# Merging VectorE instructions and taking the router's weights from a tanh, in a fused RWKV and mixture-of-experts kernel

## What is computed

```python
def step(carry, kv_t):
    aa, bb, pp = carry
    kt, vt = kv_t
    ww = u + kt
    p = jnp.maximum(pp, ww)
    e1 = jnp.exp(pp - p)
    e2 = jnp.exp(ww - p)
    y = (e1 * aa + e2 * vt) / (e1 * bb + e2)
    ww2 = pp + w
    p2 = jnp.maximum(ww2, kt)
    e1 = jnp.exp(ww2 - p2)
    e2 = jnp.exp(kt - p2)
    return ((e1 * aa + e2 * vt, e1 * bb + e2, p2), y)
# init: aa = 0, bb = 0, pp = -1e38, for each sequence
```

```python
logits = (xf @ Wr + br) / TAU            # TAU = 1.5
top_val, top_idx = jax.lax.top_k(logits, 2)
top_w = jax.nn.softmax(top_val, axis=-1)
yr = sum over the two experts of top_w * expert(x)
```

## Time and profile before

| what | before |
|---|---|
| median of 3 runs | 450.01 us (448.95 to 451.0) |
| span of the profiled execution | 471.4 us |
| busy: TensorE matmul | 399.7 us (85%) |
| busy: VectorE | 312.4 us (66%) |
| busy: ScalarE | 295.7 us (63%) |
| busy: GpSimd | 256.0 us (54%) |
| VectorE instructions | 1065 |
| mean granted TensorE clock | 0.947 of full speed |

### The profile page before, as it was taken

One profiled execution on the slowest core, in us unless ns is written; L12 is line 12 of the kernel. 1 busy time (PEld: TensorE's weight loads), 2 busy tenths in 40 slices (PEclk: granted clock), 3 DMA queues, 4 the chain that ended last, 5 costly groups with the idle time before them and its releaser, 6 DMA issues.

```text
span 471.4 us, 9935 instructions
## 1 busy us (share of the span) xinstructions
PE 399.7 (85%) x2503; PEld 307.2 (65%) x2503; DVE 312.4 (66%) x1065; ACT 295.7 (63%) x715; POOL 256.0 (54%) x328
## 2 busy tenths in 40 slices
PE   0566799998978988988593799999999999999991
PEld 0224466756746564664240369999999999999830
DVE  3799989999997997724560345656666665666162
ACT  2586699989796865663310237677777776777055
POOL 5666747567567857875566004444444444444264
PEclk9978799999999999997977699999999999999997
DMA  5389700000003000110122257876777776763394
GB/s 152 90 192 375 231 1 0 2 1 1 2 6 108 32 19 31 41 49 24 48 66 65 79 176 252 286 248 245 259 249 259 241 261 237 261 230 126 102 333 124
DMA packets 51471, 64.86 MB, mean 138 GB/s; under 512 B 8924, under 2 KB 35292, under 8 KB 51416
## 3 DMA queue, kind: packets, MB, share of 16 engines
q1 hardware_dynamic: 46968, 54.85, 35.1%
q0 software_dynamic: 4448, 9.38, 6.1%
HBM read 21.65 MB, written 13.91 MB: 75 GB/s over the span
## 4 chain that ended last, share of the span: by engine, by line
PE 51%; DVE 20%; issue 8%; SPq 6%; ACT 5%; POOL 4%; DMA 2%; another core or an unknown queue 2%; DVEq 0%; ACTq 0%; POOLq 0%
PE bank L1280 21%; PE bank L1298 11%; PE bank L987 4%; DVE rec L555 3%; DVE bst L475 2%; PE bank L969 2%; SPq L1087 2%; SPq L1086 2%; ACT z L690 2%; PE bank L1272 2%; PE bank L998 2%; PE bank L999 1%; PE bank L920 1%; POOL frs L821 1%
## 5 line engine op out<-in xcount | busy, mean ns | idle before, releaser
L1141 POOL DMA_INDIRECT routed_rows<-yo,goes_to x75 | 71.8, 957 | 112.8 <-DVE yo L1190 110.4
L1280 PE MATMUL bank<-xT,w 128*128 128x128 f32 x900 | 113.3, 276 | 0.6 <-ACT xT L1228 0.4
L1280 PEld LDWEIGHTS bank<-xT,w 128*128 128x128 f32 x900 | 106.6, 192 | 1.1 <-ACT xT L1228 0.5
L1182 DVE SCALAR_TENSOR_TENSOR actT<-bank,tile_bias,gl 128x128 f32<-128x128 f32 x225 | 65.3, 345 | 24.8 <-ACT gl L1234 15.1
L403 POOL DMA_INDIRECT dispatched_rows<-rows_all,slot_i x64 | 63.4, 990 | 22.7 <-issue 17.4
L1234 ACT ACTIVATE gl<-bank,tile_bias 128x128 f32<-128x128 f32 x225 | 65.9, 364 | 14.1 <-PE bank L1280 7.6
L1298 PE MATMUL bank<-we_sb,actT 128*128 x450 | 62.9, 276 | 1.0 <-DVE yo L1190 1.0
L1298 PEld LDWEIGHTS bank<-we_sb,actT 128*128 128x128 f32 x450 | 56.1, 192 | 1.6 <-issue 1.4
L1190 DVE SCALAR_TENSOR_TENSOR yo<-bank,goes,wb 128x128 f32<-128x128 f32 x75 | 26.3, 350 | 37.5 <-PE bank L1298 34.5
L1228 ACT ACTIVATE xT<-bank 128x128 f32<-128x128 f32 x75 | 20.8, 277 | 26.2 <-PE bank L1272 24.2
L969 PE MATMUL bank<-xk,wfk_sb 128*128 128x512 f32 x64 | 33.0, 626 | 4.9 <-DVE xk L572 3.8
(11 more groups left out here) (201 smaller groups left out, 778.4 us busy)
## 6 DMA issues: line engine op xcount, KB each, us to landing
w<-we_sb SPq DMA_DIRECT2D x75, 384.0 KB
x_all<-dispatched_rows SPq DMA_DIRECT2D x75, 68.0 KB
we_sb<-we SPq DMA_DIRECT2D x1, 4608.0 KB
rows_all<-x SPq DMA_DIRECT2D x8, 256.0 KB, 2.9
x_all<-routed_rows SPq DMA_DIRECT2D x8, 256.0 KB, 4.9
rows_all<-routed_rows SPq DMA_DIRECT2D x8, 256.0 KB, 5.3
out<-x_all SPq DMA_DIRECT2D x8, 256.0 KB, 2.5
routed_rows<-yo,goes_to POOLq DMA_INDIRECT x75
```

The lines of the kernel that those rows point to most:

```text
L1141: ng.indirect_dma_start(routed, bass.IndirectOffsetOnAxis(ap=goes_to[n // U % DB][:, n % U:n % U + 1], axis=0), yo[n % YO][:, :], None).th ...
L1182: nv.scalar_tensor_tensor(actT[n % UA][:, at], ps_a[j][:, 0:P], tile_bias[:, j, n:n + 1], gl[n % 2][:, at], ALU.add, ALU.mult).then_inc(s2 ...
L1280: return nt.matmul(to[:, 0:P], w1[m][:, off:off + P], xT[m][:, :], start=True, stop=True)
```

## The change

The change does two things. First, tiles are laid out so that pairs of operands lie side by side: the four exponentials become one tile e_all of 4x512, of which the middle two are the factors that multiply v, and the state tile ab loses its gap between the two sequences of a chunk. With that `weigh_v` issues one product of 128x1024 in place of two of 128x512, `states` issues two scans of 512 in place of four of 256 (running over the boundary between the two sequences, where the factor on the old state is zero), and `carried` issues one product of 128x1024 in place of two. Second, ScalarE takes tanh of half the difference of the logits and writes it to column DW of the rows, since the difference of the two weights is that tanh; VectorE makes W0 as 0.5 - 0.5 DW in one instruction in place of a sum, a reciprocal, a product and a difference. Nothing is moved in the order of any engine.

```diff
-        ab = tmp("ab", [P, 2, SQ, T + 1])
+        ab = tmp("ab", [P, 2, W + 1])
         gap = tmp("gap", [P, 2, W])
-        e_plus = tmp("e_plus", [P, 2, W])
-        e_minus = tmp("e_minus", [P, 2, W])
+        e_all = tmp("e_all", [P, 4, W])
+        e_plus, e_minus = e_all[:, 0:2, :], e_all[:, 2:4, :]
+        new_parts = e_all[:, 1:3, :]
...
-        e2v = tmp("e2v", [P, W])
-        new_v = tmp("new_v", [P, W])
+        weighed = tmp("weighed", [P, 2, W])
+        new_v, e2v = weighed[:, 0, :], weighed[:, 1, :]
...
             v.wait_ge(s["rel_ready"], b + 1)
-            routed_by(nv.tensor_scalar(total[:, 0:m], rel[:, 0:m], 1.0, None, ALU.add))
-            routed_by(nv.reciprocal(rows_all[:, lo:hi, W0], total[:, 0:m]))
-            routed_by(nv.tensor_tensor(w_second[:, 0:m], rel[:, 0:m], rows_all[:, lo:hi, W0], ALU.mult))
-            nv.tensor_tensor(rows_all[:, lo:hi, DW], w_second[:, 0:m], rows_all[:, lo:hi, W0], ALU.subtract)
+            nv.tensor_scalar(rows_all[:, lo:hi, W0], rows_all[:, lo:hi, DW], -0.5, 0.5, ALU.mult, ALU.add)
             v.wait_ge(s["prefix_ready"], b + 1)
...
-            nc.scalar.activation(rel[:, 0:m], fall[:, 0:m], ACT.Exp, scale=1.0 / TAU).then_inc(s["rel_ready"], 1)
+            lo, hi = BATCH[b][0] * CT, BATCH[b][1] * CT
+            nc.scalar.activation(rows_all[:, lo:hi, DW], fall[:, 0:m], ACT.Tanh, scale=0.5 / TAU).then_inc(s["rel_ready"], 1)
...
-                nv.tensor_tensor(e2v[:, :], new_in_state, pv[:, :], ALU.mult)
-                nv.tensor_tensor(new_v[:, :], new_in_output, pv[:, :], ALU.mult).then_inc(s["ev_ready"], 1)
+                nv.tensor_tensor(weighed[:, :, :], new_parts, under(pv[:, :], 2), ALU.mult).then_inc(s["ev_ready"], 1)
...
-                for q in range(SQ):
-                    at = slice(q * T, (q + 1) * T)
-                    nv.tensor_tensor_scan(ab[:, 0, q, 1:T + 1], old_in_state[:, at], e2v[:, at], 0.0, ALU.mult, ALU.add)
-                    last = nv.tensor_tensor_scan(ab[:, 1, q, 1:T + 1], old_in_state[:, at], new_in_state[:, at], 0.0,
-                                                 ALU.mult, ALU.add)
-                last.then_inc(s["states_ready"], 1)
+                nv.tensor_tensor_scan(ab[:, 0, 1:W + 1], old_in_state, e2v, 0.0, ALU.mult, ALU.add)
+                nv.tensor_tensor_scan(ab[:, 1, 1:W + 1], old_in_state, new_in_state, 0.0, ALU.mult, ALU.add).then_inc(s["states_ready"], 1)
...
-                for n in range(2):
-                    last = nv.tensor_tensor(by_sequence(nd[:, n, :]), ab[:, n, :, 0:T], by_sequence(old_in_output), ALU.mult)
-                last.then_inc(s["nd_ready"], 1)
+                nv.tensor_tensor(nd[:, :, :], ab[:, :, 0:W], under(old_in_output, 2), ALU.mult).then_inc(s["nd_ready"], 1)
```

More of the change, by code:

```diff
@@ L134, in build @@
         fall = sb("fall", [P, BT])
-        rel = sb("rel", [P, BT])
-        total = sb("total", [P, BT])
-        w_second = sb("w_second", [P, BT])
         slot = sb("slot", [P, K, BT])
@@ L416, in attention_vector @@
             nv.memset(pp[:, :, 0:1], NEG)
-            nv.memset(ab[:, :, :, 0:1], 0.0)
+            nv.memset(ab[:, :, 0:1], 0.0)
             nv.memset(ones_bf[:, :], 1.0)
@@ L872, in add_new @@
                 ng.tensor_tensor(nd[:, 1, :], nd[:, 1, :], new_in_output, ALU.add).then_inc(s["den_half"], 1)
-                ng.tensor_tensor(nd[:, 0, :], nd[:, 0, :], new_v[:, :], ALU.add).then_inc(s["den_ready"], 1)
+                ng.tensor_tensor(nd[:, 0, :], nd[:, 0, :], new_v, ALU.add).then_inc(s["den_ready"], 1)
             def residual(c):
```

## The result

The changed kernel takes 452.21 us (median of 6 runs, 450.84 to 454.61), the kernel before 450.15 us on the same chip (6 runs, 448.95 to 451.13). The ratio is 1.0052, with an interval of 1.0030 to 1.0075: slower by about half a per cent, or 2.1 us, where 449.6 was predicted.

A forecast was written before the change was run, and what follows sets the result against it. No single engine was taken to bound the chunks before the experts: TensorE to 73 us, both TensorE and VectorE to 101.2, then VectorE fuller. 1.35 + 1.2 - 2.1 = 0.45 us gained, 450.01 to 449.6 us; range 446.8 to 452.2.

The forecast's parts named there:

- Part 1: Eight VectorE instructions a chunk become four: 0.07 us a merge, 2.1 us over eight chunks, 1.35 us on the path.
- Part 2: In placed, one VectorE instruction for four saves 0.64 us in each of four batches; 1.2 us counts.
- Its split over the batches: Gain from the tanh in placed: 0.3 us at batch 0, 0.3 at 1, 0 at 2, 0.64 at 3.
- pricing the loads at about nothing: Four ScalarE table loads go, 5.1 us, but are hidden by other waits: 0, with a bound of 1.3 us.
- Part 3: Longer scans hold off GpSimd's third norm at chunks 0, 2, 4 and 5: 2.1 us lost, bounds 0 and 3.3.
- The covers that I named: Slack hiding part of the third norm's delay after chunk 0: 0.3 us left at chunk 2, 0.6 at 4, 0 at 5.
- TensorE is not waiting there: At chunk 2, the reason the third norm's delay is partly covered: 0.3 us lost.
- 32 matmuls ahead: At chunk 5, TensorE's queued work covers the third norm's delay: 0 us lost.
- (b): Wait on GpSimd counts in all three chunks, 3.3 us, against 0.6 gained: 452.7 us, slower; chance 0.18.
- (a): Wait on GpSimd costs nothing that counts: 2.55 us gained, 447.5 us, at best 446.2; chance 0.32.
- (c): Merges do nothing and the tanh alone acts, with no delay: 1.2 us gained, 448.8 us; chance 0.12.
- pauses without a releaser: Unexplained waits in the profiled execution's chain, such as 2.46 us at 228.89, said to lie all after 205 us.

The follow-up runs named there:

- free_scans: Changed kernel with scans merged in chunks 0, 2, 4 and 7 only, four of 256 in the others; 447.15 us, ratio 0.9933 to the kernel before.
- held_3: free_scans with the scans merged in chunk 3 too; 470.27 us, ratio 0.9950 to the kernel before.
- tanh_only: Kernel before with only the weights made from one tanh; 473.33 us, ratio 0.9971 to the kernel before.
- held_5: free_scans with the scans merged in chunk 5 too; 470.17 us, ratio 0.9946 to the kernel before.
- held_6: free_scans with the scans merged in chunk 6 too; 470.35 us, ratio 0.9951 to the kernel before.
- after_weigh_between: Changed kernel, all scans merged, with weigh_v moved from ahead of stats2 to behind it at two places; 452.39 us, ratio 1.0054 to the kernel before.
- scans_only: Kernel before with only its scans merged, in the changed kernel's tile layout; 479.83 us, ratio 1.0101 to the kernel before.
- held_scans: Changed kernel with scans merged in chunks 1, 3, 5 and 6 only; 454.04 us, ratio 1.0092 to the kernel before.
- held_1: free_scans with the scans merged in chunk 1 too; 471.36 us, ratio 0.9974 to the kernel before.

## Why the prediction was wrong, step by step

**Part 1, the merges**: the sizes hold nearly. Two products as one save 0.06 us (a step of 1.14 from 49.74, against twice 0.60), forecast 0.07; two scans as one save 0.03 to 0.05 (47.33 to 48.44, 1.11, against twice 0.57; from the first scan to the instruction behind the last, four take 2.32 us in `free_scans` and two 2.23 in held_3), forecast 0.06. The sum of parts 1 and 2 was 2.55 us; `free_scans`, which has all of them but the merges at four places, gains 0.67% or 3.0 us. **Part 2, the tanh**: 1.2 forecast, 1.4 measured with an interval from -0.1 to 2.9. Its split over the batches isn't borne out: by x1c of chunk 5, behind batch 0, `tanh_only` is 1.6 us ahead of the kernel before (144.52 and 146.09), where it was 0.25 ahead at chunk 4 and 0.3 was forecast for this batch. No table load came back and no wait took their place, so pricing the loads at about nothing isn't contradicted, though no run takes them away alone.

**Part 3** is the term that failed, by its second half. Its first half, that a scan holds GpSimd off for its whole length, gave 1.0 and 1.9 us for operations that took 1.02 and 1.84, and 1.2 us for a delay of 1.29. Its second half, what that delay costs, was set at 1.2, 0.3, 0.6 and 0 for the places at chunks 0, 2, 4 and 5, 2.1 in all. The traces show 1.20 at chunk 2, 1.21 at chunk 4 and 1.24 at chunk 5 (held_3, held_5, held_6), and the whole is 5.3 us by the time of chunk 7, 3.9 at the end of the same two executions, and 6.3 in the medians. The covers that I named were there: at chunk 2 the norm's delay reaches `mix` as 0.30 us. That this is the very number predicted is luck: it was set without a row. I stopped at that number. What is late next is VectorE, and GpSimd's operations over 128x512 hold VectorE off just as VectorE's scans hold GpSimd: it was enough that `mix` came 0.18 us behind GpSimd's sum instead of ahead of it. "TensorE is not waiting there" and "32 matmuls ahead" were answers about TensorE, while in these stretches VectorE was the fuller of the two, as I had read from the earlier trace rows. For chunk 5 the 0, a full cover, was wrong for the same reason: x3c waited for both of GpSimd's additions.

The Trainium skill (SBUF — State Buffer, Who interferes with whom) calls what VectorE and GpSimd share an exclusive lock. I cited it for one direction and priced that one only. Both directions are in the rows above (1.27 to 1.65 for GpSimd, 0.74 to 1.64 for VectorE), and the PSUM case of `after_weigh_between` agrees with it too.

The sum with what was measured: gains of 3.0, a loss of 3.9 to 6.3, net 0.9 to 3.3 slower; the two comparisons of the whole change gave 2.1 and 3.1. **Of the rivals**, (b) was nearest in its time (452.7) and its sign, and it named the places; but its price of 3.3 us was at most the delay of the norm in three chunks, and it was four places with the hold on VectorE added. (a) is refuted by `free_scans`, which is what (a) forecast (447.5) once the held places are taken out. (c) is refuted by `scans_only` and `held_scans`. One reading was wrong without an effect on the sum: not all pauses without a releaser lie behind 205 us, the chain of the kernel before has one of 0.84 us at 147.35. The range ended at 452.2, just under the 452.21 measured, because its upper end took in only part of (b).

**What stays open.** Between the 5.3 us at chunk 7 and the 6.3 of the medians lie what happens behind chunk 7 (the same two executions end only 3.9 apart) and the spread of the runs; they aren't told apart. The place at chunk 0, for which 1.2 us was forecast, wasn't priced: held_1 loses 2.7 us there, with a longer stretch at the low clock than `free_scans` (53.2 to 60 us against 52.5 to 55.6). Why VectorE loses even when its record starts first (by 0.02 us at chunk 0, by 0.26 in held_6) isn't shown either. The traces of before and after differ by only 1.1 us at chunk 7 (187.97 and 189.06), and before that by -1.5 at chunk 0; TensorE's stretches at 1.2 GHz fall at other moments in each kernel (at 42.7 us in the kernel before, for one, and not in the kernel after), and no run holds them fixed.

## What to carry to other kernels

Before merging VectorE instructions that read two operands from SBUF, look at what GpSimd does beside them: a merge of two scans saved about 0.05 us, and doubling the length for which GpSimd is shut out delayed the next chunk by 1.2 us at each of the three places that were measured one by one, where GpSimd carried a norm that others wait for. Merge where GpSimd is idle or busy with long work, and leave the short form where it isn't; here this gave 447.15 us against 450.42 and 453.49. And follow a delay beyond its cover: ask not only whether the next engine waits, but whether two engines that exclude each other now start in the other order.

## What the runs showed of the hardware

- The hold works both ways: of the same pair, GpSimd's sum took 1.65 us and `mix` 0.74 when VectorE led by 0.22 us, and 1.27 and 1.64 when GpSimd led by 0.18. The order of the recorded starts doesn't always tell who is held: right behind another operation of GpSimd, its addition at 55.03 in the kernel after held `mix`, recorded from 55.01 on (1.85 us).
- A VectorE instruction can be held through two operations that follow each other on GpSimd: x3c, recorded from 151.58 on in held_6, took 3.33 us, through two additions of 1.28 us (from 151.84 on). It isn't always so: in the kernel after, `mix` got in behind the first one and ended at 56.86, and GpSimd's next operation, from 56.26 on, took 1.72 us.
- Not every operation of GpSimd holds VectorE: in `free_scans` `mix` took 0.75 us (from 53.93 on) within a power of 128x4 (53.74 to 54.76), and in held_6 0.74 us (from 154.83 on) within a row scatter (154.51 to 155.76).
- A VectorE product with one operand in PSUM leaves GpSimd its full speed: 0.20 and 1.01 us beside it, 1.02 and 1.84 beside scans.
- The same kernel took 450 us in two sets of runs and 473 to 474 in two others, on other chips.
